# Moving the query-bias scores, the gate weight sums and one key load in the first pair of a fused attention kernel

## The reference

```python
x = x + xattn(layernorm(x), ctx, ctx)     # one head of 512, softmax over 1601 keys, biases bq, bk, bv
x = x + attn(layernorm(x))                # 16 heads of 32: q and k normed, sigmoid of q.k, gates
x = x + ffn(layernorm(x))                 # 8 experts, each row goes to the one with the highest logit
# in xattn:
logits = ((q @ Wq + bq) @ (k @ Wk + bk).T) / sqrt(512)
out    = softmax(logits) @ (v @ Wv + bv)
# in attn, the two gates of every row and head:
gate_q = einsum('bhtd,d->bht', q, gq);  gate_k = einsum('bhsd,d->bhs', k, gk)
```

## Time and profile before

| what | value |
|---|---|
| time, median of 3 runs | 350.5 us (349.69 to 352.65) |
| the profiled execution, its own time | 349.09 us |
| its span in the profile | 347.4 us |
| TensorE busy | 315.8 us (91% of the span) |
| VectorE busy | 161.4 us (46%) |
| ScalarE busy | 89.1 us (26%) |
| GpSimd busy | 77.6 us (22%) |
| DMA | 74.29 MB, mean 214 GB/s |

### The profile page before, as it was taken

The page is one execution under the profiler, slowest core; times in us unless marked ns, Lnnn a source line. Parts: engine busy times, 40 slices in busy tenths (PEclk is TensorE's granted clock), DMA queues, the critical chain, the costliest instruction groups (busy, mean ns, idle before and its releaser), DMA issues. The chain is left out here.

```text
span 347.4 us, 5470 instructions
## 1 busy us (share of the span) xinstructions
PE 315.8 (91%) x1940; PEld 174.8 (50%) x1940; DVE 161.4 (46%) x349; ACT 89.1 (26%) x207; POOL 77.6 (22%) x84
## 2 busy tenths in 40 slices
PE   0997988999999899999899999999999998789992
PEld 0786654743545544454554454543475577433330
DVE  3205149505463857183767437442362647034331
ACT  1233210145113463221335321152312501011010
POOL 4000012660015200221500201321325210601212
PEclk9999998899999999999999999999999999999998
DMA  7999999999999897999796999680696053730110
GB/s 252 387 351 176 184 372 359 190 190 364 298 197 300 166 158 255 298 196 354 109 169 106 352 245 234 231 358 0 235 422 252 0 184 123 222 141 31 44 41 9
DMA packets 61221, 74.29 MB, mean 214 GB/s; under 512 B 3174, under 2 KB 40070, under 8 KB 60176
## 3 DMA queue, kind: packets, MB, share of 16 engines
q1 hardware_dynamic: 59648, 69.23, 75.8%
q0 software_dynamic: 1552, 4.78, 3.9%
HBM read 70.85 MB, written 3.67 MB: 215 GB/s over the span
## 5 line engine op out<-in xcount | busy, mean ns | idle before, releaser
L1182 PE MATMUL ST<-CTX_sb,PR_sb 128*64 128x512 f32 (+1 forms) x208 | 47.7, 599 | 1.1 <-ACT PR_sb L338 1.1
L784 DVE STREAM_TRANSPOSE CT_sb<-FF_sb 128x1024 f32<-128x1024 f32 x36 | 42.4, 1220 | 11.6 <-DMA FF_sb<-ctx 10.0
L1157 PE MATMUL SC<-CT_sb,qcurP_sb 128*64 128x256 f32 x288 | 38.6, 398 | 3.3 <-DVE CT_sb L784 3.3
L1157 PEld LDWEIGHTS SC<-CT_sb,qcurP_sb 128*64 128x64 f32 x288 | 19.2, 140 | 17.9 <-issue 7.3
L1182 PEld LDWEIGHTS ST<-CTX_sb,PR_sb 128*64 128x64 f32 (+1 forms) x208 | 14.1, 136 | 24.3 <-issue 23.5
L1082 PE MATMUL A<-AW_sb,normT_sb 128*128 128x512 f32 x48 | 22.0, 600 | 0.0
L511 POOL TENSOR_TENSOR rn_sb<-ss_sb,nhalf_sb 128x16 f32<-128x16 f32 x4 | 11.6, 2905 | 35.9 <-DVE ss_sb L863 35.9
L1075 PE MATMUL TR<-ident_sb,CTX_sb 128*128 128x128 f32 (+1 forms) x128 | 15.9, 266 | 1.3 <-DVE CT_sb L331 1.1
L1125 PE MATMUL A<-AO_sb,WQK_sb 128*128 128x128 f32 (+1 forms) x64 | 16.2, 413 | 0.7 <-ACT AO_sb L611 0.7
L1075 PEld LDWEIGHTS TR<-ident_sb,CTX_sb 128*128 128x128 f32 (+1 forms) x128 | 12.9, 141 | 7.5 <-issue 5.6
L1326 PE MATMUL SC<-ident_sb 128*128 128x128 f32 x130 | 16.4, 278 | 0.0
(11 more groups left out here) (242 smaller groups left out, 489.9 us busy)
## 6 DMA issues: line engine op xcount, KB each, us to landing
CTX_sb<-ctx SPq DMA_DIRECT2D x24, 1024.0 KB, 10.4
FF_sb<-ctx SPq DMA_DIRECT2D x80, 128.0 KB, 6.9
FF_sb<-ctx SPq DMA_DIRECT2D x32, 256.0 KB, 8.0
CTX_sb<-wgu SPq DMA_DIRECT2D x4, 1024.0 KB, 9.6
CTX_sb<-wdn SPq DMA_DIRECT2D x5, 512.0 KB, 12.6
FF_sb<-wgu SPq DMA_DIRECT2D x2, 1024.0 KB, 6.2
rows<-XR_sb SPq DMA_DIRECT2D x3, 512.0 KB, 10.3
CTX_sb<-ctx SPq DMA_DIRECT2D x8, 130.0 KB
```

The source lines that it names most:

```text
L784: v.transpose(ctxT[:, pos % 2, k, :, :].rearrange("p c (b r) -> p b c r", r=Q), split[:, k, at:at + BLOCKS, :].rearrange("p b (c r) -> p b ...
L1157: last = t_.matmul(out[q, :], (qcurP if split_group else qcur)[:, c, q], ctxT[:, pos % 2, k, c, 0:n], start=(c == 0), stop=(c == DC - 1))
L1182: last = t_.matmul(ST[q, :], probs[0:w, t, q], ctxb[0:w, k, t, :], start=(t == 0), stop=(t == KT - 1))
```

## The change

Three parts, all in the first pair.

1. The matmuls of c (`query_biases`) are issued ahead of the scores of the three split groups: those of pairs 0 and 1 ahead of u = 8 (group 1), that of pair 2 ahead of u = 10 (group 2), that of pair 3 ahead of u = 12 (group 3). `c_made` is signalled behind the last.
2. The 8 gate sums leave the u-loop. Two stand right behind `shift(0)`, four behind the move of numerator chunk 1, two behind the turn of the second pair's group 1. On GpSimd `pair_bias(0)` moves from behind the 8 products to behind the second.
3. `next_split(0)` loads part 0 (groups 1 and 2 of the second pair) as soon as the first pair's groups 1 and 2 are turned, and part 1 (group 3) once group 3 is turned.

```diff
+BIAS_AT = {8: (0, 2), 10: (2, 3), 12: (3, 4)}
...
             def next_split(p):
 
+                if is_first(p):
+                    sp.wait_ge(s["keysT_made"], split_turned(0, 2))
+                    load_split(1, 0)
+                    sp.wait_ge(s["keysT_made"], split_turned(0, 3))
+                    load_split(1, 1)
+                    return
...
             for n in range(2 * DC):
+                if n == 2:
+                    pair_bias(0)
...
-            pair_bias(0)
...
-                for n in range(2 * (u - (2 * GROUPS - DC)), 2 * (u - (2 * GROUPS - DC)) + 2):
-                    if n >= 0:
-
-                        dve.wait_ge(s["gmul"], n + 1)
-                        at = HEADS * (n // DC)
-                        v.tensor_reduce(wgate[:, n % DC, at:at + HEADS], (sq, kh)[n % 2][:, :].rearrange("p (h d) -> p h d", h=HEADS),
-                                        AX.X, ALU.add).then_inc(s["gred"], 1)
             shift(0)
-            for c in range(1, NCH, 2):
-                move_numerators(dve, v.tensor_copy, 0, c)
-                turn_split(1, NEXT.groups[c // 2])
+            def gate_sums(m, n):
+                for i in range(m, n):
+                    dve.wait_ge(s["gmul"], i + 1)
+                    at = HEADS * (i // DC)
+                    v.tensor_reduce(wgate[:, i % DC, at:at + HEADS], (sq, kh)[i % 2][:, :].rearrange("p (h d) -> p h d", h=HEADS),
+                                    AX.X, ALU.add).then_inc(s["gred"], 1)
+
+            gate_sums(0, 2)
+            move_numerators(dve, v.tensor_copy, 0, 1)
+            gate_sums(2, 6)
+            turn_split(1, NEXT.groups[0])
+            gate_sums(6, 2 * DC)
+            move_numerators(dve, v.tensor_copy, 0, 3)
+            turn_split(1, NEXT.groups[1])
...
+            def query_biases(m, n):
+
+                if m == 0:
+                    pe.wait_ge(s["qk_moved"], DC + 2)
+                    pe.wait_ge(s["vec_in"], 16)
+                for p in range(m, n):
+                    for c in range(DC):
+                        last = t_.matmul(AB[1][:, p:p + 1], qpT[:, c, p * P:(p + 1) * P], vec[:, 1, c:c + 1], start=(c == 0), stop=(c == DC - 1))
+                if n == PAIRS:
+                    last.then_inc(s["c_made"], 1)
...
                     turn_keys(p, o.tile(u))
+                    if is_first(p) and u in BIAS_AT:
+                        query_biases(*BIAS_AT[u])
                     score(p, u // 2, u % 2)
...
             scores(0, {})
-            pe.wait_ge(s["qk_moved"], DC + 2)
-
-            pe.wait_ge(s["vec_in"], 16)
-            for p in range(PAIRS):
-                for c in range(DC):
-                    last = t_.matmul(AB[1][:, p:p + 1], qpT[:, c, p * P:(p + 1) * P], vec[:, 1, c:c + 1], start=(c == 0), stop=(c == DC - 1))
-            last.then_inc(s["c_made"], 1)
             bring(False, 2)
```

## The result

The changed kernel takes 348.38 us (median of 20 runs, 345.57 to 353.24), the one before 352.0 us in the same comparison (20 runs, 348.93 to 354.32); the ratio is **0.9913, 95% interval 0.9884 to 0.9941**: 0.9% or some 3 us faster, inside the range, a little less than the 3.8 us forecast, and below the 1% at which I had drawn the line. The ratio compares the means of the executions within 1.5% of the fastest of their kernel, which leaves out three of the changed kernel (351.05 to 353.24, mean granted clock 0.984 to 0.988) and one of the kernel before (354.32); over all 40 executions it is 0.993, some 2.6 us. The median itself stands 1.7 us above the forecast of 346.7; 1.5 us of that is the starting point, as the kernel before had a median of 350.5 in the three runs that I had and has 352.0 in these 20. Repeated on another chip the ratio was 0.9888 (0.9858 to 0.9917).

What follows compares the result with a forecast made beforehand. TensorE, busy 91%, was taken as the bound. Numerators at 67.4 instead of 71.20, from c moved among the scores and full-clock brings, gave 3.8 us: 349.09 to 345.3, median 346.7 us; range 345.3 to 349.6.

Steps and rivals of the forecast that it cites:

- The pass of c: First pair on TensorE: moving c's 3.6 us among the scores ends group 3's scores 1.4 us later, with c done.
- The brings at full clock: Behind the first pair's scores: the 16 bring instructions take 5.33 us instead of 7.10, 1.77 us won.
- A fall at another place: Rival, chance 0.26: the clock falls elsewhere ahead of the brings or returns later; 1.77 us lost, gain 2.0, median 348.5 us.
- The clock between 55 and 58: TensorE at groups 1 to 3: clock still low until 58, so 8 matmuls of c ahead of group 2 take 1.6 us.
- also goes: Upper bound: the first clock fall vanishes as TensorE is no longer idle ahead; about 1 us more, 4.8 in all.
- Part 2 as mere cover: Gate sums moved behind the shift: no gain alone, but without it nearly all of the 3.8 us would be gone.
- Part 3 as worth nothing on TensorE's path: Second pair's split loads: issued earlier, credited 0.7 us in landing, worth nothing on TensorE's path.
- DMA just not late at 87: Second pair's chunk 0 lands at 87.0, read at 87.1 and 87.6; it fits, 0.6 us left for the second batch.
- the 4.4 us: At the second pair's chunk 0: a gain of more than 4.4 us would stop at its landing.
- Behind the second pair's first tiles I saw no stage that would eat it.: From there on nothing takes back the gain; TensorE is the bound through pairs 1 to 3.
- that chain to the turn of qh: From late group 4 on VectorE to TensorE's turn of qh: 1.9 us of room, takes the 0.9 us delay.
- The sum: Whole kernel: 3.8 us off the profiled execution, 349.09 to 345.3, median 346.7 us.

Runs made afterwards that it cites:

- c_twice: The changed kernel with the 32 matmuls of c issued a second time behind the first pair's scores, result unused; 350.11 us, 0.9973 of the kernel before.
- gap_left: The changed kernel with no c ahead of group 1, pairs 0 and 1 ahead of group 2, 2 and 3 ahead of group 3; 348.92 us, ratio 0.9915.
- both_orders: The changed kernel with ScalarE's second query copy ahead of the route step and VectorE's turn of the next pair's second group behind it; 350.04 us, ratio 0.9953.
- the light kernel: The changed kernel loading only the first tile of the second pair's chunks 1 and 2, 3 MB less; 347.95 us, 0.9932 of the kernel before.
- no_order: The changed kernel with part 3 undone, the second pair's part 1 loaded ahead of part 0 again; 353.91 us, 1.0095 of the kernel before.
- no_sums: The changed kernel with part 2 undone, gate sums back in the u-loop and pair_bias(0) behind the 8 products; 351.52 us, ratio 1.0005.
- no_c: The changed kernel with part 1 undone, the 32 matmuls of c behind the first pair's scores; 349.48 us, 0.9973 of the kernel before.

## Why the prediction was right, and where not

- **The pass of c (term: 3.6 us less 1.4 left over).** Right in kind and place: one piece in the gap, two between the scores. What was left over is 0.27 us and not 1.4: from the first brings to the end of group 3's scores it took 26.11 us, against 25.84 before. With 3.59 us of pass gone and 1.68 us from the brings that makes 3.59 - 0.27 + 1.68 = 5.0. c_twice puts pass and clock together at 5.3 us; the prediction had 3.6 + 1.77.
- **The brings at full clock.** Right, 5.43 us against 5.33 taken. A fall at another place, to which I gave a chance of 0.26, is seen in one of the nine profiled executions with c in this place; that is too few to say whether 0.26 was fair.
- **The clock between 55 and 58** was the mis-sized term, and it is why 1.4 us were left over in the sum. I kept the low clock of the earlier trace rows in the sum, 1.6 us for 8 matmuls of c and slow scores, and put "also goes" at a bound of 4.8 us. In the profiled execution it was gone, those 8 took 1.05 us, and 5.0 us were won instead of 3.8. That it goes is not due to the filled gap as far as shown: gap_left kept the gap and the clock too, both_orders filled it and lost the clock.
- **Part 2 as mere cover.** Right: without it the ratio is 1.0005. Its places behind the shift cost nothing on the path in the changed kernel, chunk 3's move at 77.69 being in time (predicted 77.0).
- **Part 3 as worth nothing on TensorE's path.** Wrong, and the failing step is that I costed it alone, against VectorE's wait before. Once part 1 brings TensorE 5 us forward and part 2 puts two gate sums between the turn of group 1 and numerator chunk 3's move, the old order costs 3.98 us and a clock fall: 1.0095 without it against 0.9913 with it. I had even used part 0 landing at 73.6 in the timing of the sums (it landed at 74.2) without asking what the old order would do there.
- **DMA just not late at 87.** The landings were predicted well (87.0 from 34.83; measured 52.2 from the brings, the same), and the wait was 0.52 us instead of none, as the gain was 1.2 us larger and so beyond the 4.4 us that I had named as the limit there. (The 8 us by which the split parts would land earlier at the speed of large pieces should read 9: 17 us less 3.1 MB / 386 GB/s.) But I gave one number where there is a spread: in the executions in which TensorE waited for it, it landed between 52.2 and 54.8 us from the brings.
- **"Behind the second pair's first tiles I saw no stage that would eat it."** Wrong, 1.23 us of it. I had the load of the third pair's keys nowhere in the text. They landed 96.1 us behind the first brings, against 95.5 before, though TensorE had won 4 us by step o; VectorE waited 5.33 us, and its route step, ScalarE's copies of the queries (which wait behind the route step's exponential) and TensorE's score stood in line behind it. The table under the light kernel shows the 1.23 us to be what is over 4.1 us of VectorE's wait. A smaller part, 0.31 us, went at 115.58 behind the late group 4: I had followed that chain to the turn of qh, which indeed didn't wait, and not beyond.
- **The sum** was near because two errors offset each other: 1.2 us too little won at the numerators, 2.3 us given back that the text had at nothing. 5.0 - 2.3 = 2.7 by the profiles, some 3.1 by the ratio, against 3.8. That the gain came out within 1 us of the forecast is in part luck.

What stays open: what decides whether the clock falls at 54 us, how often it does in the executions without a trace, and why the landings differ by 2 us between executions of one program.

## What to carry to other kernels

Cost an edit that frees the bound engine together with its companions: a load order that was worth nothing before can be what holds the engine once it comes 5 us earlier. Where DMA engines are full, write down the landing of each transfer and the time its reader now wants it, through to the next stretch in which they are idle; a gain larger than the smallest slack is given back there. Low-density work (one-column matmuls) is best laid between dense matmuls and not in one pass ahead of them, since here it was the dense work behind the pass that paid 1.7 us at half clock.

## What was not expected of the hardware

- A wait of TensorE of 3.2 to 4.0 us costs twice: in both kernels that had one the granted clock went from 1.00 to 0.50 and the work behind it ran at 1.2 GHz for 6 to 7 us (no_order, no_sums). The gap of 2.08 us was followed by a fall in one of three executions. In gap_left two waits of 1.73 and 0.73 us with 1.2 us of work between them were followed by 0.50 from 142 to 145.
- One-column matmuls, with TensorE busy for all of 3.6 us, were followed by the fall in three of three executions (before, no_c, c_twice), and the 16 brings behind them took 7.10 us instead of 5.43.
- The spread of the times got wider with the change: 348.93 to 354.32 before, 345.57 to 353.24 after. That a kernel which stands nearer to its DMA landings takes on their spread fits the two executions of the changed kernel, whose step o differs by 4 us, but falls of the clock can widen the spread too, and no run separates the two.
